# Attention turns both heads in their own score banks, and forms a group's values in four events 512 queries wide

## What is computed

```python
content = einsum('bqhd,bkhd->bhqk', q + u_bias, k)
pos_score = _rel_shift(einsum('bqhd,khd->bhqk', q + v_bias, p))
attn = softmax((content + pos_score) / sqrt(e), axis=-1)
ctx = einsum('bhqk,bkhd->bqhd', attn, v).reshape(b, s, e)
return ctx @ Wo + bo
```

## The kernel before

| | short job | long job | no job |
|---|---|---|---|
| rounds 4-7, 12-15, 20-23, ... 52-55 (28) | 11: 4, 12, 20, 21, 28, 30, 36, 37, 44, 46, 52 | 13: 5, 6, 7, 13, 22, 23, 29, 31, 38, 39, 45, 47, 53 | 4: 14, 15, 54, 55 |
| rounds 8-11, 16-19, 24-27, ... 56-59 (28) | 8: 16, 17, 32, 33, 48, 51, 57, 59 | 17: 8-11, 18, 19, 24-27, 34, 35, 40-43, 58 | 3: 49, 50, 56 |

## Time and profile before

### The profile page before, as it was taken

The page is one execution under the profiler, slowest core; times in us unless marked ns, Lnnn a source line. Parts: engine busy times, 40 slices in busy tenths (PEclk is TensorE's granted clock), DMA queues, the critical chain, the costliest instruction groups (busy, mean ns, idle before and its releaser), DMA issues.

```text
span 523.0 us, 9946 instructions
## 1 busy us (share of the span) xinstructions
PE 446.3 (85%) x3155; PEld 317.9 (61%) x3155; DVE 358.6 (69%) x907; ACT 268.0 (51%) x550; POOL 256.2 (49%) x272
## 2 busy tenths in 40 slices
PE   8899999999999999999777999089799797358860
PEld 7665666666767677667646999034366366247750
DVE  4987677687877787687655665566756765728872
ACT  2356567766676666766513566075444221036553
POOL 3462564457572873252143455332651664636770
PEclk9899999999999999999998999679999798559995
DMA  8499999999999900000222300640000000033205
GB/s 295 126 174 175 160 158 338 212 194 183 189 188 179 139 2 6 16 2 12 74 88 72 82 25 24 233 201 1 0 2 0 1 21 20 31 79 83 66 19 162
DMA packets 68386, 52.71 MB, mean 101 GB/s; under 512 B 3238, under 2 KB 66093, under 8 KB 67696
## 3 DMA queue, kind: packets, MB, share of 16 engines
q1 hardware_dynamic: 65360, 47.24, 46.5%
q0 software_dynamic: 2976, 4.85, 3.2%
HBM read 21.30 MB, written 32.09 MB: 102 GB/s over the span
## 4 chain that ended last, share of the span: by engine, by line
PE 66%; DVE 11%; issue 8%; POOL 5%; DMA 5%; ACT 3%; POOLq 1%; SPq 0%; DVEq 0%; ACTq 0%
PE banks L1013 13%; PE banks L1151 8%; PE banks L995 6%; PE banks L1160 6%; PE banks L1028 6%; PE banks L984 5%; PE banks L1206 3%; PE banks L990 3%; PE banks L1219 3%; PE banks L1096 2%; DVE nmax L1434 2%; DMA arena<-ct_in 2%; POOL arena L760 1%; PE banks L1143 1%; PE banks L1083 1%
## 5 line engine op out<-in xcount | busy, mean ns | idle before, releaser
L789 ACT ACTIVATE arena<-banks 128x512 f32<-128x512 f32 x128 | 76.3, 597 | 69.9 <-PE banks L1013 69.6
L782 ACT ACTIVATE work<-banks,nmax 128x512 f32<-128x512 f32 x128 | 80.7, 685 | 16.4 <-DVE nmax L1434 16.0
L1013 PE MATMUL banks<-ca,work 128*128 128x128 f32 x512 | 84.3, 288 | 3.8 <-ACT work L782 3.8
L1434 DVE TENSOR_REDUCE nmax<-banks 128x2 f32<-128x1024 f32 x64 | 78.4, 1224 | 2.2
L1013 PEld LDWEIGHTS banks<-ca,work 128*128 128x128 f32 x512 | 54.7, 142 | 36.6 <-issue 23.7
L995 PE MATMUL banks<-arena 32*128 32x512 f32 (+3 forms) x256 | 60.1, 435 | 0.0
L984 PEld LDWEIGHTS banks<-arena 32*128 32x128 f32 x256 | 41.3, 184 | 30.0 <-issue 24.5
L984 PE MATMUL banks<-arena 32*128 32x128 f32 x256 | 55.1, 295 | 0.5 <-DVE corr L1521 0.4
L1151 PE MATMUL banks<-t,arena 128*128 128x128 f32 x300 | 47.2, 295 | 3.9 <-ACT t L901 1.0
L1422 DVE COPY_PREDICATED banks<-ca,banks 128x256 f32<-128x256 uint32 x64 | 27.2, 425 | 30.0 <-PE banks L984 29.6
L1206 PE MATMUL banks<-arena 128*128 128x512 f32 x96 | 45.2, 622 | 1.2 <-POOL arena L760 1.2
(11 more groups left out here) (232 smaller groups left out, 825.5 us busy)
## 6 DMA issues: line engine op xcount, KB each, us to landing
regions<-zeros SPq DMA_DIRECT2D x15, 1040.0 KB, 18.6
regions<-zeros SPq DMA_DIRECT2D x9, 1032.0 KB, 21.9
arena<-wp_in SPq DMA_DIRECT2D x1, 4624.0 KB, 25.4
arena<-wp_in SPq DMA_DIRECT2D x1, 4494.0 KB, 16.1
arena<-ct_in SPq DMA_DIRECT2D x2, 1024.0 KB, 9.5
arena<-cb_in SPq DMA_DIRECT2D x1, 1660.0 KB, 6.9
arena<-regions SPq DMA_DIRECT2D x23, 65.0 KB, 1.9
arena<-regions SPq DMA_DIRECT2D x20, 64.5 KB, 1.9
```

The costliest lines, as they stand in the source:

```text
L782: eng.activation(prob[:, r, :], bank[r], ACT.Exp, bias=nmax[:, s % 2, jj:jj + 1]).then_inc(s_exp, 1)
L789: eng.activation(probT[:, v % 2, j0 + jj, :, i % 2 * P:(i % 2 + 1) * P], turned_in(s, jj).rearrange("p (t q) -> p t q", t=TB), ACT.Copy).t ...
L1013: mm = eng.transpose(turned_in(s, jj)[:, t * P:(t + 1) * P], prob[:, 2 * (s % 2) + jj, t * P:(t + 1) * P], ident)
L1434: eng.tensor_reduce(nmax[:, s % 2, :], pair, AX.X, ALU.max, negate=True).then_inc(count(s_fixed), 1)
```

## The change

- Head 1 is turned in its own score bank too (`turned_in` gives `bank[2 * (s % 2) + jj]`). The wait of turn(s, 1) for the copy of the step before goes; a `score` now waits for the copies of both heads of two steps ago.
- Bank `PT` is free thereby, and jobs with an odd number use it, the others `JOB` (`rank` always `JOB`).
- `probT` holds a whole group (512 queries) twice; one of the two lies in `arena2`, where `wp0` goes later. The values of a group are four events of 8 instructions of 512 columns, in the steps 8m+8 to 8m+11; steps 8m+4 to 8m+7 have none. The last group keeps a half of four events 256 wide, all in step 60, and two tiles.
- The load of `wp0` moves on SyncE's queue from between the two sets of clearing DMAs to after the values of the last group but one (step 59).
- The filler matmuls of the last jobs write to bank 4.

```diff
-        if TB <= s < STEPS - TB:
-            plan.append(("values", s // TB - 1, s % TB))
-            if (s // TB - 1) % 2 == 1 and s % TB == TB - 1:
-                plan.append(("ctx", (s // TB - 1) // 2))
+        if s >= 2 * TB and s % (2 * TB) < TB:
+            plan.append(("values", s // (2 * TB) - 1, s % TB))
+            if s % TB == TB - 1:
+                plan.append(("ctx", s // (2 * TB) - 1))
         elif s == STEPS - TB:
-            plan += [("values", STEPS // TB - 2, t) for t in range(TB)]
+            plan += [("half", t) for t in range(TB)]
...
-            return PT if jj else bank[2 * (s % 2)]
+            return bank[2 * (s % 2) + jj]
...
+        def by_turns(k):
+
+            return PT if k % 2 and jobs[k][0] != "rank" else JOB
...
-                if l == 0:
-                    eng.dma_start(wp0, wp0_in[:, :]).then_inc(s_w0, 16)
...
-            eng.wait_ge(s_pv, NHALF * TB)
+            eng.wait_ge(s_pv, LAST * TB)
+            eng.dma_start(wp0, wp0_in[:, :]).then_inc(s_w0, 16)
+            eng.wait_ge(s_pv, (LAST + 2) * TB)
...
-                        eng.wait_ge(s_pTs, 2 * (s - 2) + 1)
+                        eng.wait_ge(s_pTs, 2 * (s - 2) + 2)
...
-                    if s and jj:
-                        eng.wait_ge(s_pTs, 2 * s)
...
-                        mm = eng.matmul(CTX[HP * j:HP * (j + 1), 2 * P * hh:2 * P * (hh + 1)],
-                                        vv[:, b % 2, t, h * HP:(h + 1) * HP], probT[:, v % 2, j, t, :],
-                                        start=(t == 0), stop=(t == TB - 1))
+                        mm = eng.matmul(CTX[HP * j:HP * (j + 1), queried], vv[:, b % 2, t, h * HP:(h + 1) * HP],
+                                        probT[m % 2][:, j, t, queried], start=(t == 0), stop=(t == TB - 1))
```

More of the change, by code:

```diff
@@ L265, in build @@
         arena3 = sb("arena3", [P, 2 * 2 * TB * S])
-        probT = arena3[:, :].rearrange("p (r j t q) -> p r j t q", r=2, j=HG, t=TB)
+        probT = [v.rearrange("p (j t q) -> p j t q", j=HG, t=TB) for v in (arena2[:, 0:HG * TB * S], arena3[:, :])]
         cr2 = arena3[:, 0:WIDE_R]
@@ L324, in build @@
         lg = sb("lg", [P, NTOK * E1])
+        assert HG * TB * S <= E0 * WW0
         assert WIDE_R + max(NT0, NT1) * DW1 <= 4 * TB * S
@@ L454, in turned_in @@
         def turned_in(s, jj):
-            return PT if jj else bank[2 * (s % 2)]
-        NHALF = STEPS // TB
+            return bank[2 * (s % 2) + jj]
+        LAST = B * NG - 1
         def place_of_step(s):
@@ L467, in build @@
         n_early = len(early)
-        job_bank = [early[j[0]] if k < n_early else JOB for k, j in enumerate(jobs)]
+        def by_turns(k):
+            return PT if k % 2 and jobs[k][0] != "rank" else JOB
+        job_bank = [early[j[0]] if k < n_early else by_turns(k) for k, j in enumerate(jobs)]
         by_act = ("wqT", "fold", "zT", "cxT", "wo")
@@ L784, in _ @@
                     s, jj = w
-                    _, _, v, i, j0 = place_of_step(s)
+                    b, g, _, i, j0 = place_of_step(s)
+                    m = NG * b + g
                     eng.wait_ge(s_pT, 2 * s + jj + 1)
-                    if v >= 2:
-                        eng.wait_ge(s_pv, TB * (v - 1))
-                    eng.activation(probT[:, v % 2, j0 + jj, :, i % 2 * P:(i % 2 + 1) * P], turned_in(s, jj).rearrange("p (t q) -> p t q", t=TB),
+                    if m >= 2:
+                        eng.wait_ge(s_pv, TB * (m - 1))
+                    eng.activation(probT[m % 2][:, j0 + jj, :, i * P:(i + 1) * P], turned_in(s, jj).rearrange("p (t q) -> p t q", t=TB),
                                    ACT.Copy).then_inc(s_pTs, 1)
@@ L793, in _ @@
                     i = slice(tiles_of(w)[0] * P, (tiles_of(w)[-1] + 1) * P)
-                    eng.wait_ge(s_pv, TB * (2 * m + 1 + half_of[0] if half_of else 2 * (m + 1)))
+                    eng.wait_ge(s_pv, TB * parts(m, half_of))
                     if m:
@@ L1016, in _ @@
                         warm(1, CTX[:, 0:2 * P])
-                elif kind == "values":
-                    v, t = w
-                    m, hh = divmod(v, 2)
+                elif kind in ("values", "half"):
+                    m, t = w if kind == "values" else (LAST, w[0])
+                    queried = slice(0, S if kind == "values" else S // 2)
                     b, g = divmod(m, NG)
                     if t == 0:
-                        eng.wait_ge(s_pTs, 2 * TB * (v + 1))
+                        eng.wait_ge(s_pTs, 4 * TB * (m + 1) - (2 * TB if kind == "half" else 0))
                         eng.wait_ge(*after("v", b))
-                        if m and hh == 0:
+                        if m:
                             eng.wait_ge(s_cx, m)
@@ L1033, in _ @@
                     i = w[0]
-                    v, b, g = STEPS // TB - 1, B - 1, NG - 1
+                    b, g = B - 1, NG - 1
                     eng.wait_ge(s_pTs, 2 * (STEPS - TB) + 4 * (i - 1))
@@ L1040, in _ @@
                             mm = eng.matmul(CTX[HP * j:HP * (j + 1), i * P:(i + 1) * P], vv[:, b % 2, t, h * HP:(h + 1) * HP],
-                                            probT[:, v % 2, j, t, i % 2 * P:(i % 2 + 1) * P],
+                                            probT[LAST % 2][:, j, t, i * P:(i + 1) * P],
                                             start=(t == 0), stop=(t == TB - 1))
@@ L1047, in _ @@
                     bk = job_bank[k]
-                    bk_name = early[name] if k < n_early else bank[late[jobs[k]]] if jobs[k] in late else JOB
+                    bk_name = early[name] if k < n_early else bank[late[jobs[k]]] if jobs[k] in late else by_turns(k)
                     at_bank = next(n for n in range(8) if bank[n] is bk_name)
@@ L1133, in _ @@
                     for n in filler.get(jobs[k], ()):
-                        warm(1, PT[:, 0:n])
+                        warm(1, bank[4][:, 0:n])
             def experts(l, nt, F):
@@ L1498, in _ @@
                         if a[0] >= 2:
-                            eng.wait_ge(s_pv, (a[0] - 1) * 2 * NG * TB)
+                            eng.wait_ge(s_pv, (a[0] - 1) * NG * TB)
                         eng.wait_ge(s_vset, 2)
```

## The result

The change makes the kernel slower: 536.38 us (median of 4 runs, 531.18 to 537.82) against 522.84 for the kernel before (520.18 to 524.83), a ratio of 1.024, 95% interval 1.018 to 1.030. The profiled execution took 537.82 us (span 535.9) for 524.83 (span 523.0). Forecast were 530.3 us and a range of 519 to 537: the sign held, and the range by 0.6 us (two of the four runs took 537.8); the rise is 13.5 us where 6.8 were forecast.

The account below looks back on a forecast made before the run. TensorE's queue was taken to bound the attention loop. Its work falls by 8 us but waits of 12 replace it: +4.1, plus smaller terms +2.7, is +6.8 on the median 523.55, giving 530.3 us; range 519 to 537.

Parts of the forecast that it names:

- Values at 512 columns, 1.00: TensorE's values event: fixed 0.14 plus 0.43 per 256 columns gives 1.00 us; bounds 0.57 and 1.14.
- The added wait, 1.34: Score waits for head 1's copy, so starts no sooner than 0.70 + 0.60 + 0.04 = 1.34 us after the second turn.
- the hidden copy: Rival: the copies return within the job, so only TensorE's work counts, 515.2 us; chance 0.10.
- Round lengths: Loop rounds by class, with or without values and by job: 3.14 to 4.32 us, summing to +4.1 us.
- What costs nothing: Two job banks, the removed wait, the fillers' other bank, fewer weight loads and the moved `wp0` load: no cost.
- The rival of the late load: Rival: `wp0` needs over 36 us from 247 on and delays the experts; at 40 us +4, 534.5; chance 0.04.
- TensorE's share: TensorE's busy share in the loop was to fall from 99% to some 93%.
- three signs of being wrong: Score's load sooner than 1.3 us after the second turn; rounds without values above 3.3; clock falling inside the loop.
- 4 and 5: Round 5's first turn waits for exps held up by VectorE's query work, losing round 4's saving; together -0.7 us.
- `cxT` on ScalarE: ScalarE empties this job between exps and next copies in rounds 21, 37 and 52: 0.3 x 3 = +0.9 us.
- Smaller terms: VectorE's statistics +1.0, ScalarE's emptying of `cxT` +0.9, rounds 60 and 61 +0.8; together +2.7 us.
- the clock: Rival: short idles in most rounds lower TensorE's clock; five falls in the loop add 8 us, 539; chance 0.09.

Follow-up runs that it names:

- a: Kernel before with only head 1 turned in its own score bank and the score waiting for both copies: 536.49 us, ratio 1.027.
- h: Kernel before with only the load of `wp0` moved to the end of the loop: 541.95 us for 541.08, ratio 1.003.
- d: The changed kernel with all jobs in the one bank `JOB`: 547.79 us for 541.08 of the kernel before, ratio 1.013.
- the second run of the change: The changed kernel measured once more, nothing altered, against the kernel before: 535.81 us for 524.16, ratio 1.022.
- b: The changed kernel with head 1 turned in `PT` again, earlier copy waits and one job bank: 527.6 us, ratio 1.010 against the kernel before.
- e: Wide values with head 1 in `PT`, values events in every second round and jobs moved: 532.35 us, ratio 1.008 against the kernel before.
- c: The changed kernel with filler matmuls in seven rounds without a job and behind scores 6 and 7: 533.08 us, ratio 1.022 against the kernel before.

## Why the prediction was right, and where it was not

What the runs confirm, by its steps:

- *Values at 512 columns, 1.00*: 0.99 to 1.00. The fixed part of 0.14 and the 0.43 for 256 columns hold in pairs too (1.00), and in fours (1.86).
- *The added wait, 1.34*: 1.36. Kernel a shows it alone: +11.3 us over rounds 4 to 61. Of the rivals, the hidden copy fell by this.
- *Round lengths*: with values and a long job 4.32 (4.32 forecast), a short one 4.25 (4.22), none 4.26 (4.22); without values 3.16 (3.20), 3.13 (3.14), 3.13 to 3.16 (3.14).
- *What costs nothing*: the load (h) and the job banks (d) show no cost. The rival of the late load fell: 15.6 us, not 36.
- *TensorE's share*: 93% in the loop.

That the time fell inside the range was partly luck. The median lies 0.6 us below its upper end and outside the 526 to 535 that the forecast itself stood for, and two of the three signs of being wrong that the prediction names came in part: the clock fell inside the loop, and of the rounds without values 22, 38 and 53 (3.35 to 3.37), 30 and 46 (4.08 and 4.09) and 55 (3.87) stayed above 3.3.

The forecast's +6.8 for the loop is +9.8 in rounds 4 to 61 of the run with one fall of the clock, that fall taken off (12.7 less 2.9). The difference of 3.0, class by class:

| rounds | forecast | measured |
|---|---|---|
| without values, short job (10) | -3.2 | -1.3 |
| the same, long job (12) | -8.3 | -7.8 |
| 4 and 5 | -0.7 | -0.2 |
| without values, no job (4) | +0.3 | +0.5 |
| with values, long job (17), statistics in 24 and 40 | +8.3 | +8.7 |
| with values, short job (8) | +5.2 | +5.6 |
| with values, no job (3) | +3.5 | +3.6 |
| `cxT` on ScalarE | +0.9 | in the rows above |
| 60 and 61 | +0.8 | +0.9 |

The step that failed is *Smaller terms*. It priced VectorE's statistics at steps 24 and 40, and passed over its normalising at rounds 30 and 46, which a round without values and with a short job no longer covers: 4.08 and 4.09 for 3.14, 1.9 of the 3.0. The rows for it stood in the trace of before, the same 1.48 us and the same emptied job at the same place; the forecast had listed VectorE's extra work by one kind only. The other 1.1 are hundredths in many rounds (copy wait 1.36 for 1.34; rounds with values and a long job up to 0.47 longer for 0.43).

The second miss is the clock. It was named as a rival at 0.09, with five falls and 8 us, and "the rows speak against it" was wrong: each fall cost 2.9 or 3.3 us, not 1.7, since it lasted 6.8 us and the one of the earlier trace rows 3.4, and the profiled run had two, 6.2 us. The forecast's wait and the rival came at once, and they add: 9.8 and 6.2 make the loop's 16. The chances had treated them as cases that exclude each other. The argument had compared the busy share of a whole round with one stretch of 4 us; both falls stood not in such a plain round but behind those with a longer wait (0.99 us at 40.6, and 0.78, 0.56 and 0.73 in rounds 55 and 56). Such a wait isn't enough for a fall, though: 0.97 us stood in round 5 of the kernel before and 1.00 in the second run of the change, and the clock held. The Trainium skill (TensorE: Matmul & The Clock Gate, "A second HAM failure mode: psum-queue depth-cycling") tells of another kernel, in bf16, where short idles between groups of matmuls, with PSUM banks cycled, make the clock swing between its levels. By that rule the change had to lose clock. The traces of the change, of b and of e agree, with one to several falls, and c's, with idle places filled, has none. Two traces do not agree: a idles for nearly as long as the change and has no fall between 20 and 262 us, and h has one in the queue of the kernel before. So the idles are a likely cause that no run isolates; shown is what a fall costs.

Behind the loop 2.9 of the loop's 15.8 us came back (the span is 12.9 longer). Layer 1 issues the same 631 matmul instructions in 191 us instead of 193; its falls of the clock lie elsewhere (at 412 us the granted clock was 0.50 before, at the same work after it was 0.73).

Busy time by stretch of layer 1, after, and then one stretch of it:

```profile
345.00:536.00 191.00, 132.04 (x631) 90.01 (x631) 123.59 (x392) 74.48 (x174) 94.24 (x95) 0.84 0.20 63
...
427.00:431.00 4.00, 2.14 (x6) 1.58 (x7) 3.11 (x17) 0.60 (x1) 2.62 (x4) 0.73 0.02 4
```

Whether these 2.9 us come from the shift of the start alone was only argued, not tried.

## What to carry to other kernels

A bank that is refilled at once must have its reader back before the refill: price that loop (here turn 0.70, copy 0.60, return 0.06) against the shortest work that stands behind it in any round, not the mean, before the bank is given away. If a change makes a busy engine idle in part, list every piece of work of the other engines that its length had covered, one by one, and give the clock a term of its own beside the waits. A cost that hangs on the number of shape changes is best saved without changing anything else: two visits joined in every second round gained 3.6 us by medians, 2.0 of them seen in the loop, where the wide form gave all back.

## What was not expected of the hardware

A fall of the granted clock from 1.00 to 0.50 lasted 6.8 us in the loop (43.1 to 49.9 and 237.7 to 244.5 in the trace after) and cost 3.3 and 2.9 us. In the same kernel, with round lengths that agree within 0.06 us up to that point, the first of them came in one run and not in the other. The kernel before had none in its loop in one profiled run, and h, with the same order of work on TensorE, had one of 3.4 us. The same kernel e took 524 to 540 us in ten runs. And the same program before took 522 us on one chip and 541 on another.
